# Turning the normalised rows of a macaron block by VectorE block turns and a DRAM scratch instead of on TensorE, with statistics pooled and two attention products on GpSimd

## The chip, the cores and the metric

One core of one Trainium2 chip. The metric is device time in microseconds (us) of one execution of the kernel.

## What is computed

The input x is 16 sequences of 256 rows of 128 features in float32 (4096 rows). Three blocks follow one another, each added to its own input; each begins with a norm of a row (minus its mean, times the reciprocal root of its variance plus 1e-5).

```python
x = x + 0.5 * ffn(layernorm(x))
x = x + attn(layernorm(x))
x = x + 0.5 * ffn(layernorm(x))

def ffn(x):                      # 128 -> 512 -> 512 -> 512 -> 128, weights -1, 0 or 1
    h = silu(tlin(x, w1, s1)) * tlin(x, w2, s2)
    h = gelu(tlin(h, h1, sh1))
    h = gelu(tlin(h, h2, sh2))
    return tlin(h, w3, s3)       # tlin: x @ w.T * s

def attn(x):
    h = layernorm(x) * gamma + beta
    keys, values = h @ Wk.T + bk, h @ Wv.T + bv
    w = exp((keys @ Wka.T + bka) / sqrt(128))
    w = w / cumsum(w, axis=1)
    return cumsum(w * keys, axis=1) * values
```

## The kernel before, in words

The 4096 rows are 8 tiles of 512 rows. A tile goes through the first ffn (t = 0 to 7), the attention (t = 0 to 7) and the second ffn (t = 8 to 15), so there are 16 ffn passes and 8 attention passes, and 24 norms. x is held twice in SBUF: by rows (x_sb, used for the first ffn's norms) and turned, features on the partitions (xt_sb), where all results are added. All 512-column matmuls of an ffn work on turned tiles; each product is made twice, with the rounded activation ("hi") and with the rest ("lo"), against weights that are exact.

A norm n: where the rows are only in xt_sb, TensorE turns them into y_ps (stage u, four 128x128 transposes). VectorE takes statistics of four 128-row blocks (stats, L825), combines them (aggr, L830 and L832) and makes neg_mean and veps (L839, L840). GpSimd makes rstd by a power and nmr = neg_mean * rstd (L362, L364). ScalarE writes the normalised rows z (four activations, L726). TensorE turns z into xt_ps (stage t, transpose4, L462), and ScalarE and VectorE read that bank: xn_hi (L764) and xn_lo (L913) for an ffn, h_t (L767) for attention.

An ffn pass is stage p1.0 to p1.3 (gate and up products, 4 matmuls each), p2.0 to p2.3 and p3.0 to p3.3 (8 each) and p4 (8): 88 matmuls of 512 columns. Between them ScalarE does tanh, high1, gelu2, high2, gelu3, high3 (four each; a high writes the rounded copy), VectorE gate, up (L855, L867) and low1, low2, low3 (L877, the rest after rounding), and dt adds y_ps to xt_sb (L930). p2 and p3 share two banks (hid_ps), so p3.2 can't start before gelu3.0 has read the first.

An attention pass: logits, keys and values on TensorE (L632, L629, L635) out of one bank xt_ps, which also takes the turned z; exp and keys on ScalarE (L776, L772); on VectorE cumsum (L935), two reciprocals (recip, L940), weight (wgt = kw * rcsum, L943), weight_keys (wgt * keys, L947), pool (L951), values (L957) and dt (xt_sb += adelta, L961).

Every engine runs its own list in order. The lists are strings, ORDER for the middle, walked in loops of three steps with two attention passes (a, b), with START, FIRST_STEP and LAST_STEP around them; a step is one ffn pass on TensorE, and AHEAD says for which later tile a stage of that step is. Waits are on semaphores, set inside the stages. SyncE (the queue SP) issues the loads and, from tile 8 on, the stores (L340). GpSimd has little beside its norms: the copies of the weights at the start and two of the low1 (L375).

Of the kernel before, what the change touches and what calls it, by code (L numbers as in the profile page):

```python
# [4 lines left out]
P = 128  # L5
# [27 lines left out]
        "hi:w1 hi:w2 zwait z",  # L33
        "t vec:s1 bits:h1.1 bits:h1.3 tanh.0 tanh.1 tanh.2 high1.0 tanh.3 high1.1 zwait z.0 z.1 high1.2 bits:h2.0 "
# [15 lines left out]
FIRST_STEP = {  # L50
# [6 lines left out]
}  # L57
ORDER = {
# [31 lines left out]
LAST_STEP = {  # L90
    "PE": "p2.0 p2.1 p2.2 p2.3 p4 p3.0 p3.1 p3.2 last:p4a last:p3.0 last:p3.1 last:p4b last:p4c.0 last:p4c.1",
    "ACT": "gelu2.0 gelu2.1 high2.0 high2.1 gelu2.2 high2.2 gelu2.3 high2.3 gelu3.0 high3.0 gelu3.1 high3.1 "
           "gelu3.2 high3.2 last:gelu.0 last:gelu.1",
# [905 lines left out]
```

## Time and profile before

| | before |
|---|---|
| median of 3 runs | 376.88 us (376.24 to 377.13) |
| span of the profiled execution | 374.9 us |
| left around the span, to the median | 2.0 us |
| TensorE busy | 368.0 us (98%) |
| VectorE busy | 321.9 us (86%) |
| ScalarE busy | 314.1 us (84%) |
| GpSimd busy | 52.6 us (14%) |

The profiled execution is one of its own; its time beside its span isn't listed, so the span is set against the median of the runs. Busy time is the union over an engine's instructions, and instructions overlap at their ends, so that the pace of back-to-back instructions is the distance of their starts and is shorter than the duration of one.

### The profile page before, as it was taken

How to read it: one execution, taken by the hardware profiler on the slowest of the kernel's cores; microseconds unless marked ns; L12 is line 12 of the kernel's file. 1: busy time of each engine (PE TensorE's matmuls, PEld its weight loads, DVE VectorE, ACT ScalarE, POOL GpSimd, SP SyncE). 2: the span in 40 equal slices, each digit the busy share in tenths (PEclk: the TensorE clock that was granted, in tenths of full speed). 3: DMA queues.
4: the chain of work that ended last, by engine and by line, in shares of the span. 5: the costliest groups of instructions: out<-in, count | busy, mean ns of one | idle time of the engine just before them, and what ended most of it. 6: DMA issues, size and time to landing. Idle time of an engine off the chain costs nothing.

```text
span 374.9 us, 5278 instructions
## 1 busy us (share of the span) xinstructions
PE 368.0 (98%) x1662; PEld 291.9 (78%) x1662; DVE 321.9 (86%) x713; ACT 314.1 (84%) x549; POOL 52.6 (14%) x67
## 2 busy tenths in 40 slices
PE   7999999999999999999999999999999999999996
PEld 2678888787787877778788787778877778788885
DVE  5898787999999799999988999989799999976733
ACT  4999699989977999798699979967998998686763
POOL 3531101202101202201021120102101210020000
PEclk9999999999999999999999999999999999999999
DMA  7760000000000000000000000000000000000001
GB/s 246 277 265 1 2 0 0 1 2 1 0 2 0 1 2 2 2 0 1 2 0 1 2 1 28 2 28 1 2 29 0 0 30 1 30 1 28 2 0 58
DMA packets 4494, 9.81 MB, mean 26 GB/s; under 512 B 625, under 2 KB 1905, under 8 KB 4209
## 3 DMA queue, kind: packets, MB, share of 16 engines
q1 hardware_dynamic: 3744, 8.65, 6.3%
q10 hardware_dynamic: 720, 0.80, 0.6%
q8 instruction: 15, 0.25, 0.2%
q14 instruction: 15, 0.11, 0.1%
HBM read 7.35 MB, written 2.10 MB: 25 GB/s over the span
## 4 chain that ended last, share of the span: by engine, by line
PE 95%; DMA 2%; DVE 1%; SPq 1%; issue 0%; ACT 0%; ACTq 0%
PE hid_ps L449 60%; PE gate_ps L449 8%; PE y_ps L449 7%; PE up_ps L449 7%; PE xt_ps L462 3%; DMA x_sb<-x 2%; PE y_ps L462 2%; PE xt_ps L632 2%; PE xt_ps L629 2%; PE xt_ps L635 2%; PE up_ps L507 1%; PE gate_ps L507 1%; DVE gate L855 0%; PE xt_ps L449 0%; DVE xt_sb L924 0%
## 5 line engine op out<-in xcount | busy, mean ns | idle before, releaser
L449 PE MATMUL hid_ps<-act_hi,hi_h 128*128 128x512 f32 x480 | 195.6, 408 | 0.0
L449 PE MATMUL hid_ps<-act_lo,hi_h 128*128 128x512 f32 x480 | 186.8, 389 | 0.0
L877 DVE TENSOR_TENSOR act_lo<-full,act_hi 128x512 fp32r<-128x512 f32 x185 | 122.2, 683 | 26.8 <-ACT act_hi L708 24.3
L701 ACT ACTIVATE full<-hid_ps,vec 128x512 f32<-128x512 f32 x123 | 84.4, 686 | 34.9 <-PE hid_ps L449 31.2
L449 PEld LDWEIGHTS hid_ps<-act_hi,hi_h 128*128 128x128 f32 x480 | 90.1, 188 | 22.4 <-issue 4.1
L449 PEld LDWEIGHTS hid_ps<-act_lo,hi_h 128*128 128x128 f32 x480 | 90.2, 188 | 22.1 <-issue 4.3
L708 ACT ACTIVATE act_hi<-full 128x512 fp32r<-128x512 f32 x127 | 78.5, 630 | 2.3
L362 POOL TENSOR_TENSOR rstd<-veps,half 128x4 f32<-128x4 f32 x24 | 35.2, 1467 | 272.5 <-DVE veps L840 272.5
L855 DVE SCALAR_TENSOR_TENSOR gate<-tanh,gate_ps 128x512 f32<-128x512 f32 x60 | 40.6, 679 | 9.2 <-ACT tanh L684 8.6
L684 ACT ACTIVATE tanh<-gate_ps,s_half 128x512 f32<-128x512 f32 x60 | 40.8, 686 | 8.2 <-PE gate_ps L449 8.2
L867 DVE SCALAR_TENSOR_TENSOR full<-up_ps,s_half,gate 128x512 f32<-128x512 f32 x60 | 44.2, 742 | 0.9
L689 ACT ACTIVATE act_hi<-full 128x512 fp32r<-128x512 f32 x60 | 37.3, 621 | 0.2
L940 DVE RECIPROCAL rcsum<-csum 128x256 f32<-128x256 f32 x16 | 27.9, 1743 | 0.0
L449 PE MATMUL gate_ps<-xn_hi,hi_w 128*128 128x512 f32 x59 | 24.7, 419 | 0.0
L726 ACT ACTIVATE z<-y_ps,nmr,rstd 128x128 f32<-128x128 f32 x64 | 24.0, 460 | 0.8 <-POOL nmr L364 0.8
L449 PE MATMUL y_ps<-act_hi,hi_w 128*128 128x512 f32 x60 | 24.2, 403 | 0.0
L449 PE MATMUL y_ps<-act_lo,hi_w 128*128 128x512 f32 x60 | 23.5, 392 | 0.0
L449 PE MATMUL gate_ps<-xn_lo,hi_w 128*128 128x512 f32 x59 | 23.0, 390 | 0.0
L449 PE MATMUL up_ps<-xn_lo,hi_w 128*128 128x512 f32 x59 | 23.0, 390 | 0.0
L449 PE MATMUL up_ps<-xn_hi,hi_w 128*128 128x512 f32 x59 | 23.0, 390 | 0.0
L825 DVE BATCH_NORM_STATS2 stats<-y_ps 128x6 f32<-128x128 f32 x64 | 14.2, 285 | 0.0
L462 PE MATMUL xt_ps<-ident,z 128*128 128x128 f32 x90 | 13.6, 273 | 0.0
(159 smaller groups left out, 397.8 us busy)
## 6 DMA issues: line engine op xcount, KB each, us to landing
xt_sb<-xt SPq DMA_DIRECT2D x1, 2048.0 KB, 10.9
out<-xt_sb SPq DMA_DIRECT2D x7, 256.0 KB, 2.0
x_sb<-x SPq DMA_DIRECT2D x1, 1536.0 KB, 6.6
raw_h<-h2t SPq DMA_DIRECT2D x4, 256.0 KB, 7.3
raw_h<-h1t SPq DMA_DIRECT2D x2, 256.0 KB, 5.9
raw_w<-w2t ACTq DMA_DIRECT2D x1, 256.0 KB, 4.0
raw_w<-w1t SPq DMA_DIRECT2D x1, 256.0 KB, 3.8
raw_h<-h1t ACTq DMA_DIRECT2D x1, 256.0 KB, 6.7
```

The costliest lines, as they stand in the source:

```text
L362: eng.tensor_tensor(rstd[:, :], veps[:, :], half[:, :], ALU.pow).then_inc(s_pow, 1)
L449: mm = eng.matmul(ps, w, a, start=(first and n == 0), stop=(last and n == len(seq_) - 1))
L462: mm = eng.transpose(dst[:, j * P:(j + 1) * P], src[:, j * P:(j + 1) * P], ident[:, :])
L684: eng.activation(tanh_b[m % 2][:, :], gate_home(T, m)[:, :], ACT.Tanh, scale=s1_half[:, m:m + 1]).then_inc(s_tanh, 1)
L689: eng.activation(act_hi[first_act(T)][:, m, :], full1[m % 2][:, :], ACT.Copy).then_inc(s_hi[1], 1)
L701: eng.activation(full23[m % 2][:, :], home23(n, T, m)[:, :], ACT.Gelu, scale=col("sh1" if n == 2 else "sh2", m)).then_inc(s_gelu[n], 1)
L708: eng.activation(act_hi[n][:, m, :], full23[m % 2][:, :], ACT.Copy).then_inc(s_hi[n], 1)
L726: zz = eng.activation(z[:, j * P:(j + 1) * P], norm_blk(kind, t, j), ACT.Identity, bias=nmr[:, j:j + 1], scale=rstd[:, j:j + 1])
L855: eng.scalar_tensor_tensor(gate_b[m % 2][:, :], tanh_b[m % 2][:, :], 1.0, gate_home(T, m)[:, :], ALU.add, ALU.mult).then_inc(s_gate, 1)
L867: eng.scalar_tensor_tensor(full1[m % 2][:, :], up_home(T, m)[:, :], s12_half[:, m:m + 1], gate_b[m % 2][:, :], ALU.mult, ALU.mult).then_in ...
L877: eng.tensor_tensor(act_lo[a][:, m, :], full[m % 2][:, :], act_hi[a][:, m, :].bitcast(F32), ALU.subtract).then_inc(s_lo[n], 1)
L940: eng.reciprocal(rcsum[:, b], csum[:, b]).then_inc(s_rc, 1)
```

## The change

Of the 24 norms, the first three (ffn 0, 1, 2: BY_PE) stay as they were. For the other 21 (13 of an ffn, 8 of attention):

- stage t of TensorE is gone. VectorE turns z in 32x32 blocks into a buffer zt (stage turn, one instruction of 128x512). SyncE then stores zt (256 KB) in a DRAM scratch, waits for it, and reads it back by four DMAs, one for 32 features each, that put the blocks where they belong: the runs are 32 numbers, 128 bytes, 512 of them in each DMA. ScalarE's and VectorE's stages t read the result xnt from SBUF. zt, the scratch and xnt have two buffers.
- the statistics are combined on GpSimd (aggregate): seven small instructions of 128x4 or 128x8, ahead of the power.
- all eight attention passes: weight is kw * keys and is done on GpSimd, weight_keys multiplies it by rcsum on VectorE, and dt (xt_sb += adelta) is done on GpSimd.
- the lists of all engines are written out for each of 16 steps, and GpSimd and SyncE have one too; stages stand in other places than before. The stores stand in SyncE's list between the turns.

```diff
+            def turn(kind, t):                       # SyncE
+                i, use = slot(kind, t)
+                eng.wait_ge(s_turn, turn_of[kind, t] + 1)
+                if use > 0:
+                    eng.wait_ge(s_turned[i], 64 * use)
+                eng.dma_start(turns[i], zt_b[i][:, :]).then_inc(s_parked[i], 16)
+                if use > 0:
+                    before, at = by_dma[turn_of[kind, t] - 2]
+                    eng.wait_ge(*((s_xlo, at) if before == "ffn" else (s_ht, at + 1)))
+                eng.wait_ge(s_parked[i], 16 * (use + 1))
+                blocks = turns[i].rearrange("(s c) (j q r) -> q c j s r", c=32, j=SUB, r=32)
+                for b in range(4):
+                    eng.dma_start(xnt_b[i][32 * b:32 * b + 32, :].rearrange("c (j s r) -> c j s r", j=SUB, r=32),
+                                  blocks[b]).then_inc(s_turned[i], 16)
...
+            def aggregate(n):                        # GpSimd
...
+                eng.wait_ge(s_bn, SUB * n + SUB)
+                eng.tensor_tensor(pair_diff[:, :], stats[:, :, 1], stats[:, :, 4], ALU.subtract).then_inc(s_agg, 1)
+                eng.tensor_tensor(pair_sum[:, :, :], stats[:, :, 1:3], stats[:, :, 4:6], ALU.add).then_inc(s_agg, 1)
+                eng.wait_ge(s_agg, done + 1)
+                eng.tensor_tensor(diff_sq[:, :], pair_diff[:, :], pair_diff[:, :], ALU.mult).then_inc(s_agg, 1)
+                eng.wait_ge(s_agg, done + 2)
+                eng.tensor_scalar(var_part[:, :], pair_sum[:, :, 1], a / P, b, ALU.mult, ALU.add).then_inc(s_agg, 1)
+                eng.wait_ge(s_agg, done + 3)
+                eng.tensor_scalar(diff_part[:, :], diff_sq[:, :], a / 4.0, None, ALU.mult).then_inc(s_agg, 1)
+                eng.tensor_scalar(neg_mean[:, :], pair_sum[:, :, 0], -0.5, None, ALU.mult).then_inc(s_agg, 1)
+                eng.wait_ge(s_agg, done + 5)
+                eng.tensor_tensor(veps[:, :], var_part[:, :], diff_part[:, :], ALU.add).then_inc(s_ve, 1)
...
+                elif stage == "att_weight":          # GpSimd
+                    eng.wait_ge(s_keysb, t + 1)
+                    eng.wait_ge(s_wgk, t + 1)
+                    eng.tensor_tensor(wgt[:, :], kw[:, :], keys[:, :], ALU.mult).then_inc(s_wg, 1)
+                elif stage == "att_dt":              # GpSimd
+                    eng.wait_ge(s_adelta, t + 2)
+                    eng.tensor_tensor(xt_tile(t), xt_tile(t), adelta[:, :], ALU.add).then_inc(s_x2, 1)
...
+                elif stage in ("turn", "att_turn"):  # VectorE
+                    i, use = slot(kind, t)
+                    eng.wait_ge(s_za, norm_of[kind, t] + 2)
+                    if use > 0:
+                        eng.wait_ge(s_parked[i], 16 * use)
+                    eng.transpose(zt_b[i][:, :], z[:, :]).then_inc(s_turn, 1)
...
+                elif stage == "t" and t not in BY_PE:    # ScalarE
+                    i, use = slot("ffn", t)
+                    eng.wait_ge(s_p1, MC * t)
+                    eng.wait_ge(s_turned[i], 64 * (use + 1))
+                    eng.activation(xn_hi[:, :], xnt_b[i][:, :], ACT.Copy).then_inc(s_xhi, 1)
```

The lists of step 1, and VectorE's of step 11 (a stage without a number before it is for the tile that AHEAD gives: z, turn and stats for step + 2, p1, tanh and high1 for step + 1; "a0:" is attention pass 0):

```diff
+    SP     "turn"
+    POOL   "norm"
+    PE     "t 0:p3.2 p1.0 p1.1 0:p3.3 p2.0 p2.1 p4 p2.2 p1.2 p2.3 a0:u p1.3 p3.0 p3.1 p3.2"
+    ACT    "z gelu2.0 0:high3.3 gelu2.1 high2.0 gelu2.2 tanh.2 high2.1 high2.2 gelu2.3 high2.3 high1.0 tanh.3 "
+           "3:t high1.1 gelu3.0 high3.0 gelu3.1 high1.2 high3.1 a0:z gelu3.2 3:tanh.0 high3.2 high1.3 3:tanh.1 "
+           "gelu3.3 high3.3"
+    DVE    "gate.0 0:low3.2 gate.1 turn 0:low3.3 up.0 low2.0 dt up.1 gate.2 low2.1 low2.2 low2.3 a0:stats 3:t "
+           "low1.0 up.2 low3.0 gate.3 low1.1 up.3 a0:turn 4:stats low3.1 low1.2 low1.3 low3.2"
...
+    DVE    "a5:pool a5:values gate.0 dt gate.1 up.0 stats up.1 low2.0 low2.1 a6:cumsum a6:recip.0 turn a7:stats "
+           "low1.0 low2.2 low2.3 gate.2 a6:recip.1 up.2 a7:turn low1.1 gate.3 low3.0 up.3 13:t a6:weight_keys "
+           "low1.2 low3.1 low1.3 a6:pool low3.2 a6:values low3.3"
```

## Rows read from the trace of the kernel before

**Rows 1.** The page's head and first part: busy time of each engine.
```profile
span 374.9 us, 5278 instructions
PE 368.0 (98%) x1662; PEld 291.9 (78%) x1662; DVE 321.9 (86%) x713; ACT 314.1 (84%) x549; POOL 52.6 (14%) x67
```

**Rows 2.** Waits of TensorE, first and last of four: us in total, times, longest.
```profile
PE y_ps L642 <- POOL ident L355: 2.1, 1, 2.1
...
PE gate_ps L507 <- ACT act_hi L689: 0.2, 1, 0.2
```

**Rows 3.** The chain that ended last, us 59.84 to 84.85: start, us, what.
```profile
62.56 1.81 PE hid_ps L449 x8
...
65.29 0.44 PE xt_ps L462 x4
65.72 1.85 PE y_ps L449 x8
...
68.50 0.86 PE xt_ps L632 x2
...
79.38 0.45 PE xt_ps L462 x4
79.82 0.44 PE y_ps L462 x4
80.26 3.66 PE hid_ps L449 x16
```

**Rows 4.** Stretch 60 to 320 us: busy time of each engine (instructions), clock, DMA.
```profile
60.00:320.00 260.00, 260.00 (x1168) 207.05 (x1167) 240.71 (x525) 229.19 (x396) 36.65 (x38) 1.00 0.01 5
```

**Rows 5.** Groups by line and shape: busy us, mean ns of one, idle before.
```profile
L940 DVE RECIPROCAL rcsum<-csum 128x256 f32<-128x256 f32 x16 | 27.9, 1743 | 0.0
L943 DVE TENSOR_TENSOR wgt<-kw,rcsum 128x512 f32<-128x512 f32 x8 | 5.4, 676 | 0.0
L375 POOL TENSOR_TENSOR act_lo<-full,act_hi 128x512 fp32r<-128x512 f32 x2 | 2.6, 1296 | 2.2 <-ACT act_hi L689 2.2
```

**Rows 6.** Timeline of VectorE, us 257.9 to 263: start, us of each piece.
```profile
257.89 0.38 DVE L832 BATCH_NORM_AGGREGATE mv<-stats 128x2 f32<-128x6 f32 x4
...
259.64 0.16 DVE L839 TENSOR_SCALAR neg_mean<-mv 128x4 f32<-128x4 f32 x1
259.71 0.16 DVE L840 TENSOR_SCALAR veps<-mv 128x4 f32<-128x4 f32 x1
259.78 0.68 DVE L877 TENSOR_TENSOR act_lo<-full,act_hi 128x512 fp32r<-128x512 f32 x1
...
261.27 1.88 DVE L877 TENSOR_TENSOR act_lo<-full,act_hi 128x512 fp32r<-128x512 f32 x3
```

**Rows 7.** Timeline of GpSimd, us 258 to 270.
```profile
259.95 1.38 POOL L362 TENSOR_TENSOR rstd<-veps,half 128x4 f32<-128x4 f32 x1 [19.87 <-DVE veps L840]
261.41 0.60 POOL L364 TENSOR_TENSOR nmr<-neg_mean,rstd 128x4 f32<-128x4 f32 x1
268.19 1.01 POOL L362 TENSOR_TENSOR rstd<-veps,half 128x4 f32<-128x4 f32 x1 [6.18 <-DVE veps L840]
269.27 0.20 POOL L364 TENSOR_TENSOR nmr<-neg_mean,rstd 128x4 f32<-128x4 f32 x1
```

**Rows 8.** Timeline of VectorE, us 14 to 20, while GpSimd did L375.
```profile
18.45 1.00 DVE L877 TENSOR_TENSOR act_lo<-full,act_hi 128x512 fp32r<-128x512 f32 x1 [0.26 <-POOL act_lo L375]
```

**Rows 9.** SyncE's store L340 and load L330: ns of the issue min/median/max.
```profile
L340 SPq DMA_DIRECT2D out<-xt_sb x7: 332/332/348, 230.2 to 368.2; - x7
DMA to landing us min/median/max: 2.0/2.0/2.2
L330 SPq DMA_DIRECT2D raw_w<-w3t x1: 657/657/657, 6.0 to 6.0; - x1
```

**Rows 10.** ScalarE's queue of DMAs: whole page, then us 5.0 to 5.4 (packets, MB, share).
```profile
q10 hardware_dynamic: 720, 0.80, 0.6%
q10 hardware_dynamic: 46, 0.01, 10.8%
```

More of the change, by code:

```diff
@@ L49 @@
 )
-FIRST_STEP = {
[6 rows of a table removed]
-}
-ORDER = {
[5 rows of a table removed]
+STEPS = {
+    "SP": (
+        "",
+        "turn",
+        "a0:turn turn",
+        "a1:turn turn",
+        "turn",
+        "a2:turn turn",
+        "a3:turn turn",
+        "turn",
+        "a4:turn turn",
+        "a5:turn store turn",
+        "store turn",
+        "a6:turn store turn",
+        "a7:turn store turn",
+        "store turn",
+        "store",
+        "store",
+    ),
+    "POOL": (
+        "norm",
+        "norm",
+        "a0:norm norm",
+        "a1:norm norm",
+        "a0:weight norm",
+        "a2:norm a0:dt a1:weight norm",
+        "a3:norm a2:weight a1:dt norm",
+        "a2:dt norm",
+        "a4:norm a3:weight a3:dt norm",
+        "a4:weight a5:norm norm",
+        "a4:dt norm",
+        "a5:weight a6:norm a5:dt norm",
+        "a7:norm a6:weight a6:dt norm",
+        "a7:weight a7:dt norm",
+        "",
+        "",
+    ),
[18 rows of a table added]
     ),
     "ACT": (
[10 rows of a table removed]
[43 rows of a table added]
     ),
     "DVE": (
-        "a:stats low2.0 a:aggr t a:veps low2.1 gate.0 up.0 gate.1 up.1 low2.2 gate.2 low1.0 low2.3 dt up.2 low1.1 "
-        "stats gate.3 aggr up.3 veps a:cumsum low3.0 a:recip.0 low1.2 low3.1 low1.3 low3.2 a:recip.1 low3.3",
-        "b:stats a:weight b:aggr t b:veps a:weight_keys low2.0 a:pool gate.0 a:values gate.1 low2.1 a:dt up.0 up.1 "
[6 rows of a table removed]
-    ),
-}
[L90 to L93, printed above, removed]
-    "DVE": "low2.0 low2.1 low2.2 low2.3 low3.0 low3.1 dt low3.2 last:dt.0 last:dt.1",
-}
[39 rows of a table added]
+    ),
+}
 POOL_FIRST = ("norm", 1, 2)
-AHEAD = {"stats": 2, "aggr": 2, "veps": 2, "norm": 2, "zwait": 2, "z": 2, "t": 1, "p1": 1, "tanh": 1, "gate": 1,
-         "up": 1, "high1": 1, "low1": 1, "u": 2, "p4": -1, "dt": -1}
+BY_PE = (0, 1, 2)
+AGGREGATE = 3
+AHEAD = {"stats": 2, "aggr": 2, "veps": 2, "norm": 2, "z": 2, "t": 1, "p1": 1, "tanh": 1, "gate": 1,
+         "up": 1, "high1": 1, "low1": 1, "u": 2, "turn": 2, "p4": -1, "dt": -1, "store": -1}
 def macaron_block(nc, x, xt, w1t, w2t, h1t, h2t, w3t, wkt, wkat, wvt, wkn, vecs, out, seq):
@@ L111, in macaron_block @@
     assert D == P and TOK % seq == 0
-    GROUP, ATT = 3, 2
-    FIRST = 2
-    LOOPS = NT // ATT
-    assert FIRST + GROUP * LOOPS + 2 == 2 * NT
+    assert all(len(steps) == 2 * NT for steps in STEPS.values())
     with ExitStack() as ctx:
@@ L140, in macaron_block @@
         z = sb("z", [P, TOK])
+        zt_b = [sb(f"zt_{i}", [P, TOK]) for i in range(2)]
+        xnt_b = [sb(f"xnt_{i}", [P, TOK]) for i in range(2)]
+        turns = nc.dram_tensor("turns", [2, P, TOK], F32).ap()
         xn_hi = sb("xn_hi", [P, TOK], F32R)
@@ L314, in macaron_block, with schedule, step @@
         block = ctx.enter_context(nc.Block())
+        def schedule(engine, emit, part):
+            def step(i, order):
+                for stage, chunk, t in items(order, i):
+                    emit(stage, chunk, t)
+            if part == "start":
+                step(-1 if engine == "PE" else -2, START[engine][0])
+            if part == "first":
+                step(-1, START[engine][1])
+            if part == "second":
+                step(0, SECOND_LAYER)
+            if part == "rest":
+                for i, order in enumerate(STEPS[engine]):
+                    step(i, order)
         @block.sync
@@ L336, in _, with emit @@
             eng.dma_start(xt_sb[:, :], xt).then_inc(s_xt, 16)
-            for t in range(NT - 1):
-                eng.wait_ge(s_x1, NT + t + 1)
-                eng.dma_start(out[:, t * TOK:(t + 1) * TOK], xt_tile(t)).then_inc(s_out, 16)
+            def turn(kind, t):
[12 more added lines that the diff above has]
+                                  blocks[b]).then_inc(s_turned[i], 16)
+            def emit(stage, chunk, t):
+                if stage in ("turn", "att_turn"):
+                    turn("ffn" if stage == "turn" else "att", t)
+                elif stage == "store":
+                    eng.wait_ge(s_x1, t + 1)
+                    eng.dma_start(out[:, (t - NT) * TOK:(t - NT + 1) * TOK], xt_tile(t)).then_inc(s_out, 16)
+            schedule("SP", emit, "rest")
             for h in range(2):
@@ new lines, in emit @@
+            def emit(stage, chunk, t):
+                if stage in ("norm", "att_norm"):
+                    norm(norm_of["ffn" if stage == "norm" else "att", t])
+                elif stage == "att_weight":
[5 more added lines that the diff above has]
+                    eng.tensor_tensor(xt_tile(t), xt_tile(t), adelta[:, :], ALU.add).then_inc(s_x2, 1)
@@ L434, in _ @@
+            schedule("POOL", emit, "rest")
         @block.tensor
@@ L584, in emit @@
                         p23(int(stage[1]), t, chunk, general)
-                    elif stage in ("t", "att_t"):
-                        n = norm_of["ffn" if stage == "t" else "att", t]
+                    elif stage == "t":
+                        n = norm_of["ffn", t]
                         if n == 0:
@@ L613, in emit @@
                         last_p4_end(chunk)
-                    elif stage == "u" and t >= NT:
+                    elif stage == "u":
                         eng.wait_ge(s_x2, t - NT + 1)
```

163 lines of the change are left out of this document (85 added, 78 removed), and 123 rows, old and new, of tables (FIRST_STEP, ORDER, STEPS).

## The prediction

> **What bounds the kernel now.** I read the page's busy times first: TensorE is busy for 368.0 of 374.9 us, the others have 14% and more left [rows 1]. Busy matmuls are modelled and can hide gaps, so I looked at its waits next: four entries, 3.5 us in all, from the warm-up products (L642) to the second layer of the first tile (L507) [rows 2]. Third, the chain that ended last: between 60 and 85 us it is TensorE without a break [rows 3]; there an ffn product of 8 matmuls takes 1.81 us, so the 88 of a pass take 20 us, and four 128x128 turns take 0.44 to 0.45 us. The reader is to see that each piece starts where the one before ends. So TensorE's queue sets the time, and work taken off it counts in full, as long as nothing else makes it wait. The middle shows how much room there is: of 260 us VectorE is busy 240.7 (93%) and ScalarE 229.2 (88%), and TensorE all the time at a granted clock of 1.00 [rows 4]. Room of 7% on an engine with a fixed order is little: what I add to VectorE's or ScalarE's waits beyond that shows up in TensorE.
>
> **Part 1, TensorE's turns.** 21 of 24 groups of four transposes go, 84 in all. A group is 0.44 to 0.45 us in the chain, and the product behind it takes 1.85 instead of 1.81 us [rows 3], so 0.48 us if that is its doing. 21 x 0.44 = 9.2, 21 x 0.48 = 10.1. I take 9.7 us off. Stage u (turning xt_sb into rows, 16 groups) stays. Nothing else on TensorE gets cheaper: the 1,408 products of the ffn passes and the attention's are the same. So 9.7 us is also about all that can be had.
>
> **Part 2, VectorE.** Per norm it loses four aggregates with a memset (0.38 us) and two small instructions (0.14 us by their starts, 259.64 to 259.78) [rows 6], some 0.55 us. Per attention pass it loses two instructions of 128x512 with two SBUF inputs, like weight's 676 ns [rows 5], at a pace of 0.6 us when back to back (1.88 us for three) [rows 6]. 21 x 0.55 + 16 x 0.6 = 21.2 us off. It gains 21 block turns of 128x512. The trace has no such instruction. Lower bound: the pace of one pass over 512 columns, 0.6 us [rows 6]. Upper bound: the slowest row, the reciprocal, 1743 ns for 256 columns [rows 5], so 3.5 us for 512. A turn reads and writes each number once without arithmetic, so it is nearest to the plain passes: I take 0.65 us, 13.7 us in all. VectorE ends at 321.9 - 21.2 + 13.7 = 314 us of about 365, 86% as before. At the upper bound it would have 60 us more, 374, and be the bound itself.
>
> In the steps where attention is dense it is tighter. Before, two attention passes fall on three steps; a step is then 20.0 + 2 x 0.45 + 0.67 x (3 x 0.86 + 0.9) = 23.2 us of TensorE [rows 3], and VectorE has 93% of it, 21.5 us. By the new lists steps 5 to 12 hold 6.5 passes in 8 steps, 0.81 per step; TensorE's length of a step there is 20.0 + 0.45 + 0.81 x (3 x 0.86 + 0.45) = 22.9 us (0.86 is one attention product, 0.45 a stage u [rows 3]). One pass costs VectorE roughly 10 us (an estimate: reciprocals 3.5, four scans, statistics and four products), so it has 21.5 + 0.14 x 10 - 0.81 x 1.2 = 21.9 us, 96%. It fits, with under 1 us per step to spare.
>
> **Part 3, GpSimd.** Seven small instructions per norm, like nmr: 0.20 us alone, 0.60 when it must share with VectorE [rows 7]; with the power (1.0 to 1.4) and nmr the chain from statistics to z is 7 x (0.2 to 0.35) + 1.4 + 0.3 + waits of some 0.5 = 3.6 to 4.7 us. Before it was 0.5 (VectorE) + 1.7. So z can be written 2 us later. The new lists leave from the end of stats to z at least 3 VectorE instructions and a step's boundary (3 us), mostly 6 us and more. In about five norms ScalarE will wait some 1 us at z. Behind z in its queue are gelu2 and high2 of the tile on TensorE; TensorE has a product of 1.8 us in each of two banks as cover. The two moved products cost 1.30 us each on GpSimd [rows 5]: 16 x 1.3 = 21 us, and GpSimd ends near 53 + 21 + 21 x 2.2 = 120 us, a third of the span. Behind adelta's dt is stage u of the next norm or a store, one pass later than before; wgt is needed half a step later. I cost these at nothing; TensorE's own products cover them.
>
> What GpSimd does to VectorE: while the first of its 1.3 us products ended, a low took 1.00 us in place of 0.68 [rows 8]; beside the power three lows ran at 0.6 us each [rows 6, 7]. So at most 0.3 us for each of the 16 large products, 5 us of VectorE's 51 us room, and nothing for the small ones. The Trainium skill (SBUF — State Buffer, section SBUF: two separate sides) says more: a GpSimd instruction and a VectorE one with two SBUF inputs exclude each other for a whole instruction. By that rule each large product could cost VectorE 1.3 us, 21 us in all, still under its room in the sum; the rows for the small instructions show only GpSimd stretched.
>
> **Part 4, the way through DRAM.** It replaces 0.45 us on TensorE by a delay: block turn, store, read back. The store is like the output's: 2.0 us from issue to landing for the same 256 KB [rows 9]. Then four issues of 0.33 to 0.66 us each [rows 9], and the last lands 2.0 us after its issue if its 512 packets of 128 bytes cost what bytes do. Bounds of a packet: 46 packets, almost all of the 88-byte rows of vecs, took 10.8% of 16 engines in 0.4 us, 15 ns each; all 720 of that queue, 1.1 KB on average, took 0.6% of 374.9 us, 50 ns [rows 10]. At 15 ns the 2048 packets are 1.9 us on 16 engines and hide behind the issues; at 50 ns they are 6.4 us. A turn is then 2.0 + 3 x 0.5 + 2.0 and 0.7 for semaphores and SyncE = 6.2 us, or at the upper end 2.0 + 6.4 + 2.0 = 10.4 us. I take 6.2: the small packets are the nearest row.
>
> What it must fit into: ScalarE's instructions between z and t of the same norm (z as 4). Tile 3: 12; over the 21 norms I count 11 once, 12 three times, 13 four times, then 14 to 27. ScalarE did 396 instructions in 260 us [rows 4], 0.66 us each, so 7.2 us at the least, less 0.65 for the block turn: 6.6 us for a turn of 6.2. It fits even there, if VectorE is on time; in 13 norms there are 2 us and more. Where it doesn't, ScalarE stands at t, and behind it high1 and gelu3, for which p3.2 waits.
>
> **Sum.** The profiled span of 374.9 stands 2.0 us under the median. 376.9 - 9.7 = 367.2. For the waits of parts 2 to 4 (eight tight turns, five tight z, the dense steps), I add 1.5 us, of a range of 0 to 4: **368.7 us**. Own range of this case: 366.3 to 371.5.
>
> **Rivals.** (a) The gain is there but a third or more of it goes into waits of ScalarE and VectorE in the dense steps, where orders are full: 5 to 9 us lost, 371.5 to 376.1. For it: 96% of VectorE. Against: before, 93% left TensorE without any wait [rows 2, 4]. (b) Slower: packets are at the upper end. A turn of 10.4 us exceeds the eight tight places by 10.4 + 0.65 - (11 to 13) x 0.66, 2.5 to 3.8 us each, 25 us, and five others by some 4 us. ScalarE has 12% of room, and half of it, 14 us, reaches TensorE: 376.9 - 9.7 + 14 = 381 us. It decides from some 10 us per turn on, where half the excess passes 9.7 us. The Trainium skill (VectorE: DVE Perf Modes, section The three transpose paths) warns of just this: a plain strided DMA used as a transpose is 19 times slower than the hardware's. Here that would be, from the store's 256 KB in some 0.7 us of moving, 13 us per read-back and well over 400 us in all. Its case is a large innermost stride; here 32 numbers lie together on both sides, and [rows 10] shows 88-byte packets at 15 ns. (c) VectorE becomes the bound: from 1.2 us per block turn on in the dense steps, from 3.1 us everywhere; at 3.5 us about 380 to 385. Against: nothing that only moves data is so slow [rows 5, 6]. (d) The transposes were hidden anyway and nothing changes: against it is the unbroken chain [rows 3].
>
> **Chances.** Forecast 60%; (a) 18%; (b) 12%, a quarter of it within 0.2% of before; (c) 5%; another wait in the new orders that costs over 10 us 3%; under 366.3 us 2%. About 0.2% is what a measurement can tell from no change. Faster 0.80, same 0.04, slower 0.16. Range 366.3 to 376.1: the forecast and (a).
>
> **What would show it.** After, TensorE's busy time is near 358 of a span of 366.7. Right: 12 transposes of z left beside the 64 of xt_sb, VectorE's block turn near 0.65 us, VectorE's busy time near 314, GpSimd's near 120, read-backs landing about 2 us after issue, four of 0.33 to 0.66 us. Wrong, and how: TensorE's hid_ps waiting for ScalarE, which waits for a DMA at its t (b), for GpSimd's nmr at z (part 3), or for VectorE's low (a, c). The prediction falls if TensorE's products themselves slow down, which nothing in the trace suggests.

## The result and the profile after

The median of before is 377.0 us (4 runs), that of after 379.12 us (4 runs, 378.63 to 379.98): a ratio of 1.0061, 95% interval 1.0044 to 1.0078. The change made the kernel 2.1 us slower, where 368.7 us was forecast, and the time is outside the range. The profiled execution of after took 378.93 us, with a span of 377.1 us.

The head and busy times of after, to be held against [rows 1]:

```profile
span 377.1 us, 5304 instructions
PE 365.9 (97%) x1578; PEld 281.0 (75%) x1578; DVE 319.9 (85%) x571; ACT 311.6 (83%) x549; POOL 111.8 (30%) x230
```

The 84 transposes are gone (1662 matmuls, now 1578), but TensorE's busy time fell by 2.1 us and not by 9.7. The ends of matmuls are modelled, so lost time hides in it. The distances between the starts of TensorE's instructions show it: summed over what is beyond the pace of each kind, from 20 us on, they lose 2.7 us before and 13.8 us after (worked out from the two timelines). That is 11.1 us of new gaps, more than the transposes were worth. (An instruction's pace is the usual distance from its start to the next one's; for an ffn matmul it is 0.227 us.) In windows of 20 us the loss is seen even in busy time (before, TensorE was busy for 20.00 us in each of these three):

```profile
60.00:80.00 20.00, 19.13 (x83) 14.73 (x82) 14.91 (x29) 17.16 (x30) 7.03 (x21) 1.00 0.21 41
260.00:280.00 20.00, 18.89 (x82) 14.10 (x80) 18.23 (x33) 17.04 (x29) 6.32 (x12) 1.00 0.19 53
280.00:300.00 20.00, 18.90 (x78) 13.81 (x78) 18.00 (x31) 16.91 (x29) 8.36 (x18) 1.00 0.24 53
```

The granted clock (third column from the end) is 1.00 as in [rows 4], so it is no cause. The waits of all engines in after (us, times, longest):

```profile
ACT full L862 <- PE hid_ps L609: 19.9, 34, 1.9
ACT z L894 <- POOL nmr L552: 15.8, 17, 1.6
DVE zt L1083 <- ACT z L894: 12.3, 10, 2.3
...
PEld hid_ps L609 <- ACT full L862: 7.2, 12, 1.4
PEld hid_ps L609 <- DVE act_lo L1052: 4.0, 10, 0.5
...
ACT h_t L938 <- DMA xnt<-turns: 1.2, 1, 1.2
```

The second line is the new one. Before, ScalarE stood at z for nmr for 1.4 us in all. Now it stands there 17 times, 15.8 us (16 times and 15.2 us at the 21 changed norms; the other wait, 0.6 us, is at the first norm and was there before), and VectorE stands 12.3 us at its block turn for the z that is then late. The first line is ScalarE's cover: before, it had 31.2 us of waits for TensorE; 11 us of them are used up. The last line is all that ScalarE waits for the DRAM route.

The groups and the DMAs of after (busy us, mean ns; KB each, us from issue to landing):

```profile
L1052 DVE TENSOR_TENSOR act_lo<-full,act_hi 128x512 fp32r<-128x512 f32 x185 | 123.7, 695 | 27.8 <-ACT act_hi L869 23.2
L532 POOL TENSOR_TENSOR pair_diff<-stats 128x4 f32<-128x4 f32 x21 | 8.0, 382 | 114.2 <-DVE stats L1000 114.1
L550 POOL TENSOR_TENSOR rstd<-veps,half 128x4 f32<-128x4 f32 x24 | 27.5, 1144 | 10.6 <-DVE veps L1015 7.8
L1083 DVE STREAM_TRANSPOSE zt<-z 128x512 f32<-128x512 f32 x21 | 14.9, 707 | 12.4 <-ACT z L894 12.3
...
turns<-zt SPq DMA_DIRECT2D x21, 256.0 KB, 2.0
xnt<-turns SPq DMA_DIRECT2D x84, 64.0 KB, 2.5
```

**One late z, followed.** The timeline of after around tile 4's norm, GpSimd's and ScalarE's, then TensorE's (start, us):

```profile
57.51 0.58 POOL L532 TENSOR_TENSOR pair_diff<-stats 128x4 f32<-128x4 f32 x1 [3.12 <-DVE stats L1000]
58.04 0.65 POOL L533 TENSOR_TENSOR pair_sum<-stats 128x8 f32<-128x8 f32 x1
58.65 0.64 POOL L535 TENSOR_TENSOR diff_sq<-pair_diff 128x4 f32<-128x4 f32 x1
59.38 0.51 POOL L537 TENSOR_SCALAR var_part<-pair_sum 128x4 f32<-128x4 f32 x1
59.97 0.23 POOL L539 TENSOR_SCALAR diff_part<-diff_sq 128x4 f32<-128x4 f32 x1
60.17 0.22 POOL L540 TENSOR_SCALAR neg_mean<-pair_sum 128x4 f32<-128x4 f32 x1
60.35 0.21 POOL L542 TENSOR_TENSOR veps<-var_part,diff_part 128x4 f32<-128x4 f32 x1
60.69 1.04 POOL L550 TENSOR_TENSOR rstd<-veps,half 128x4 f32<-128x4 f32 x1
61.81 0.20 POOL L552 TENSOR_TENSOR nmr<-neg_mean,rstd 128x4 f32<-128x4 f32 x1
```
```profile
62.04 1.65 ACT L894 ACTIVATE z<-x_sb,nmr,rstd 128x128 f32<-128x128 f32 x4 [1.42 <-POOL nmr L552]
63.60 0.67 ACT L862 ACTIVATE full<-hid_ps,vec 128x512 f32<-128x512 f32 x1
```
```profile
63.06 0.39 PE L609 MATMUL hid_ps<-act_lo,hi_h 128*128 128x512 f32 x1
64.32 0.50 PE L609 MATMUL hid_ps<-act_hi,hi_h 128*128 128x512 f32 x1 [0.87 <-ACT full L862]
```

The statistics were done at 57.43. Seven small instructions, the power and nmr take until 62.01, 4.58 us. ScalarE had nothing else to do from 60.62 and stood 1.42 us at z. Behind z in its list is a gelu, which starts at 63.60 and frees the bank; TensorE starts its product at 64.32, 1.03 us behind its pace of 0.23 us. So 1.03 us of the 1.42 us at z come out at TensorE within one product.

**All of them.** For each of the 21 norms I took two times from the timelines of after: the chain, from the end of stats to the end of nmr, and the room, from the end of stats to where ScalarE stands at z. In 16 norms the room is 2.6 to 4.4 us, mean 3.5, and the chain 3.0 to 5.4 us, mean 4.2. Three more (room 5.9 to 12.9 us) are fine. In the last two, a weight stands ahead of the norm in GpSimd's list and waits for keys; z waits 1.63 and 1.04 us there.

### The profile page after: what moved, and what is told of

It is laid out like the page before. It is cut to its first block and busy times, and to the rows that moved or that the text cites. A ratio compares the mean times of both kernels' runs of the same rounds, so it can differ in the third digit from the quotient of the medians.

```text
span 377.1 us, 5304 instructions
## 1 busy us (share of the span) xinstructions
PE 365.9 (97%) x1578; PEld 281.0 (75%) x1578; DVE 319.9 (85%) x571; ACT 311.6 (83%) x549; POOL 111.8 (30%) x230
## 3 DMA queue, kind: packets, MB, share of 16 engines
q1 hardware_dynamic: 51120, 19.67, 19.4%
## 5 line engine op out<-in xcount | busy, mean ns | idle before, releaser
L609 PE MATMUL hid_ps<-act_hi,hi_h 128*128 128x512 f32 x480 | 192.0, 400 | 2.2 <-ACT full L862 2.2
L1052 DVE TENSOR_TENSOR act_lo<-full,act_hi 128x512 fp32r<-128x512 f32 x185 | 123.7, 695 | 27.8 <-ACT act_hi L869 23.2
L532 POOL TENSOR_TENSOR pair_diff<-stats 128x4 f32<-128x4 f32 x21 | 8.0, 382 | 114.2 <-DVE stats L1000 114.1
L550 POOL TENSOR_TENSOR rstd<-veps,half 128x4 f32<-128x4 f32 x24 | 27.5, 1144 | 10.6 <-DVE veps L1015 7.8
L609 PE MATMUL gate_ps<-xn_hi,hi_w 128*128 128x512 f32 x59 | 26.0, 440 | 0.0
L1083 DVE STREAM_TRANSPOSE zt<-z 128x512 f32<-128x512 f32 x21 | 14.9, 707 | 12.4 <-ACT z L894 12.3
L588 POOL TENSOR_TENSOR xt_sb<-xt_sb,adelta 128x512 f32<-128x512 f32 x8 | 10.7, 1341 | 47.6 <-DVE adelta L1141 47.6
```

What stands on the lines that cost most here:

```text
L550: eng.tensor_tensor(rstd[:, :], veps[:, :], half[:, :], ALU.pow).then_inc(s_pow, 1)
L609: mm = eng.matmul(ps, w, a, start=(first and n == 0), stop=(last and n == len(seq_) - 1))
L1052: eng.tensor_tensor(act_lo[a][:, m, :], full[m % 2][:, :], act_hi[a][:, m, :].bitcast(F32), ALU.subtract).then_inc(s_lo[n], 1)
L1083: eng.transpose(zt_b[i][:, :], z[:, :]).then_inc(s_turn, 1)
```

## The experiments

Seventeen kernels ran. Theory A of the expectations is the late z: the chain on GpSimd is longer than the room, and the lists have no slack behind z. Its rivals are the way through DRAM, the two products moved to GpSimd with what they cost VectorE, and the fullness of VectorE and ScalarE. "Gaps" is TensorE's loss worked out as above (before 2.7, after 13.8 us); "z" is ScalarE's wait at z for nmr.

| run | median us | ratio to before (95%) | z us | gaps us |
|---|---|---|---|---|
| after | 379.12 | 1.0061 (1.0044 to 1.0078) | 15.8 | 13.8 |
| e1 statistics on VectorE | 373.36 | 0.9907 (0.9892 to 0.9922) | 0.4 | 7.7 |
| e2 short chain | 369.97 | 0.9812 (0.9799 to 0.9826) | 2.6 | 5.5 |
| e3 z and turn later | 386.80 | 1.0273 (1.0247 to 1.0299) | 1.5 | 21.8 |
| e4 products on VectorE | 386.22 | 1.0245 (1.0231 to 1.0259) | 14.8 | 21.6 |
| e5 two small ones on VectorE | 376.82 | 0.9997 (0.9982 to 1.0013) | 10.1 | 10.5 |
| e6 four on VectorE | 374.20 | 0.9925 (0.9911 to 0.9940) | 4.1 | 8.9 |
| e7 two more small ones | 388.05 | 1.0309 (1.0280 to 1.0338) | 23.7 | 22.0 |
| e8 e2 with stage u doubled | 377.78 | 1.0025 (1.0015 to 1.0035) | 1.1 | 3.5 |
| e9 before, statistics on GpSimd | 376.93 | 1.0004 (0.9995 to 1.0014) | 1.6 | 3.1 |
| e10 turn later | 388.03 | 1.0289 (1.0245 to 1.0333) | 13.4 | 22.1 |
| e11 z one later | 378.55 | 1.0045 (1.0031 to 1.0059) | 3.4 | 13.2 |
| e12 low with one input | 369.61 | 0.9807 (0.9792 to 0.9822) | 5.0 | 5.0 |
| e13 no wait for the store | 378.51 | 1.0052 (1.0037 to 1.0067) | 15.6 | 13.3 |
| e14 e1 with e13 | 373.32 | 0.9899 (0.9880 to 0.9918) | 0.6 | 7.7 |
| e15 e2 with e13 | 369.02 | 0.9805 (0.9789 to 0.9821) | 1.5 | 3.9 |
| e16 stats earlier | 377.20 | 1.0020 (1.0009 to 1.0031) | 12.5 | 12.0 |
| e17 e16, norm before weight | 376.38 | 0.9993 (0.9984 to 1.0003) | 9.7 | 10.7 |

### The chain on GpSimd, longer and shorter

**e1** puts the statistics back on VectorE, for all 21 norms; the arithmetic is complete.

```diff
-                if n >= AGGREGATE:               # GpSimd
-                    aggregate(n)
+                if n >= AGGREGATE:               # VectorE, behind stats
+                    norm_aggr(n)
+                    norm_veps(n)
```

> The statistics of the 21 later norms are combined on VectorE again (four aggregates, neg_mean, veps right behind stats, two buffers for each); all else is the changed kernel's, 379.1 us. Theory A, the chain: seven small instructions on GpSimd take 1.5 us alone and up to 4 us when each waits for a VectorE product, so that z comes some 1 us late at 15 norms, ScalarE stands there, and TensorE after it; without them z is on time: 371 to 374 us, ScalarE's waits at z under 3 us (15.8 before). Theory B, full lists: VectorE and ScalarE have no room in the dense steps, and VectorE gets 11 us more here: 380 us or more.

373.36 us, 5.8 us faster than after and 3.5 faster than before, with VectorE busier (329.5 us) than in either. The chain is 2.1 to 2.6 us in all norms but three, against the same rooms.

**e2** makes the chain three small instructions. It leaves out of the variance the part that comes from the difference of the two half-rows' means.

```diff
-                eng.tensor_tensor(pair_diff[:, :], stats[:, :, 1], stats[:, :, 4], ALU.subtract)
...
-                eng.tensor_tensor(veps[:, :], var_part[:, :], diff_part[:, :], ALU.add).then_inc(s_ve, 1)
+                eng.tensor_scalar(veps[:, :], pair_sum[:, :, 1], a / P, b, ALU.mult, ALU.add).then_inc(s_ve, 1)
```

> GpSimd makes only three of the seven small instructions of each norm (the sum of the halves, neg_mean, veps); the part of the variance that comes from the difference of the halves' means is left out. VectorE and ScalarE do the same as in the changed kernel. Theory A: the chain is 1 to 2 us shorter, 372 to 375 us, waits at z under 4 us. Theory B: nothing was taken off a full engine, 378 us or more.

369.97 us, near the forecast of 368.7 and below the 372 to 375 us that theory A gave for this run. Its busy times and its two waits around z:

```profile
PE 360.6 (98%) x1578; PEld 282.4 (77%) x1578; DVE 318.1 (86%) x571; ACT 311.6 (85%) x549; POOL 91.6 (25%) x146
```
```profile
DVE zt L1076 <- ACT z L887: 3.9, 7, 1.2
ACT z L887 <- POOL nmr L545: 2.6, 5, 1.2
```

In the 16 tight norms the chain is 3.05 us on average and the room as before, 3.5. Four instructions fewer are worth 9.2 us, everything else being the same: the lists, the route, the block turns, the moved products.

**e5 and e6** take two (difference and sum of the halves) and four of the seven to VectorE, the arithmetic complete. **e7** adds two small instructions to the seven, whose results nothing uses.

```diff
+                for of in (extra_a, extra_b):        # e7, GpSimd
+                    eng.tensor_tensor(of[:, :], stats[:, :, 1], stats[:, :, 4], ALU.subtract)
```

> Complete statistics; of the seven small instructions the first two (difference and sum of the halves) are made by VectorE right behind stats, five stay on GpSimd, and the power and nmr behind them. The changed kernel is 379.1, the short chain (three small ones) 370.0 us. Theory A, each GpSimd instruction in the chain costs some 2.3 us of the whole: 374 to 376 us. Theory B, room on VectorE counts most: it gets 3 us more, so 379 us or more.

> Complete statistics; four of the small instructions (sum, difference, neg_mean, the part of the variance within the halves) are VectorE's, three stay on GpSimd. Theory A: the chain on GpSimd is as long as in the short chain, VectorE has some 6 us more, 370 to 372.5 us, less than with all statistics on VectorE (373.4) and below the kernel before (376.75). Theory B: 373.5 us or more.

> The changed kernel with two more small instructions at the head of GpSimd's chain (the difference made three times). Theory A: another 3 to 6 us, 382 to 385 us. If the chain is not what decides: 379 us.

The waits at z go 4.1, 10.1, 15.8, 23.7 us for three, five, seven and nine small instructions on GpSimd, and the time 374.2, 376.8, 379.1, 388.1 us. The order is theory A's; its sizes are not. e5 came out above the 374 to 376 us expected, e7 above the 382 to 385, and e6 in the range that was theory B's, 373.5 us or more. Only e2 and e7 change the chain and nothing on VectorE: each of the four that e2 leaves out is worth 2.3 us over 21 norms, each of the two that e7 adds 4.5 us, where z is already late. e6 and e2 leave the same number on GpSimd; the four that e6 does on VectorE (9 us more, 327.1 against 318.1) cost 4.2 us. That is about the price of VectorE's fullness here; 1.5 us more of waits at z are in it.

### Is the saving on TensorE there at all?

**e8** is e2 with each group of four transposes of stage u done twice: 16 groups, 7.0 us more on TensorE by [rows 3].

```diff
+                        for j in range(SUB):
+                            eng.transpose(y_ps[:, j * P:(j + 1) * P], xt_tile(t)[:, j * P:(j + 1) * P], ident[:, :])
                         transpose4(y_ps, xt_tile(t), s_u)
```

> The short chain (370.0 us) with the four transposes of stage u made twice, 16 groups of 0.44 us more on TensorE. If TensorE's queue sets the time again once the chain is short: 7 us more, 376.5 to 377.5 us. If waits still do: 371 to 374 us.

7.8 us slower than e2, where 7.0 were added and 376.5 to 377.5 us expected; the 0.8 us over is not explained. With z in time, TensorE's queue sets the time as before, and its instructions count in full.

### The moved products

**e4** gives weight and att_dt back to VectorE and keeps the rest.

```diff
-        "a2:norm a0:dt a1:weight norm",              # GpSimd's list
+        "a2:norm norm",
```

> The two attention products (weight and dt) are back on VectorE, weight right before weight_keys, dt right behind values; statistics stay on GpSimd. Theory C, large GpSimd products block VectorE (one low took 1.60 us beside one): 16 blocks of up to 0.9 us go, 9.6 us of VectorE work come: about 379 us. Theory A: z waits remain, 379 to 381 us. Theory B: VectorE is fuller, 382 us or more.

386.22 us: the moved products are not the cause of the loss but worth 7 us where they are. That is theory B's range (382 us or more); A and C had given 379 to 381. The waits at z stay (14.8 us). TensorE's for lows grow, from 4.0 and 3.4 us to 6.4 and 6.1. Busy time alone doesn't explain the 7 us: e1, with z in time, has VectorE busy for 329.5 us and takes 373.36 us, e4 328.7 and 386.22. How much of it is the late z and how much the place of the two products in VectorE's list was not tested.

### The same chain on the old lists

**e9** is the kernel before with nothing but the aggregate of the change on GpSimd.

> One part alone: the kernel before, with its lists and its turns on TensorE, and only the statistics of norms 3 to 23 combined on GpSimd (seven small instructions, as in the changed kernel). Theory A, the chain: it is 2 to 4 us longer than the 1.7 us that these lists were made for; z and what is behind it in ScalarE's list come late: 380 to 388 us, waits at z over 10 us (1.4 before). If the chain hurts only together with the way through DRAM: 376 to 378 us, since VectorE gets 11 us of room.

```diff
             def norm_aggr(n):                        # and norm_veps alike
+                if n >= AGGREGATE:                   # GpSimd does aggregate(n) ahead of the power
+                    return
```

No difference, where theory A had forecast 380 to 388 us. The forecast took the chain of these lists for 1.7 us. That is GpSimd's part of it; the trace of before, read as above, has 3.0 to 7.9 us from the end of stats to the end of nmr (mean 5.0), because aggr and veps stand behind other instructions in VectorE's list. One of these norms (VectorE, GpSimd twice, ScalarE):

```profile
69.81 0.87 DVE L825 BATCH_NORM_STATS2 stats<-x_sb 128x6 f32<-128x128 f32 x4
...
72.19 0.16 DVE L840 TENSOR_SCALAR veps<-mv 128x4 f32<-128x4 f32 x1
```
```profile
72.43 1.31 POOL L362 TENSOR_TENSOR rstd<-veps,half 128x4 f32<-128x4 f32 x1 [10.25 <-DVE veps L840]
73.82 0.57 POOL L364 TENSOR_TENSOR nmr<-neg_mean,rstd 128x4 f32<-128x4 f32 x1
```
```profile
77.47 1.64 ACT L726 ACTIVATE z<-x_sb,nmr,rstd 128x128 f32<-128x128 f32 x4
```

The chain is 3.7 us here and the room 6.9. Over the 21 norms of before the room is 4.1 to 15.2 us, mean 6.5. In e9 the chain is 3.1 to 4.7 us, mean 3.9, about as in after; the shortest rooms are two of 4.1 us, the next five 4.4 to 4.7, and z waits 1.6 us in all. So theory A holds only with its second half. The chain alone costs nothing, and it is not longer than before's was; what the change took away is the room, from 6.5 us on average to 3.5 in 16 norms. e9 also says that taking 21 aggregates off VectorE (314.3 us) gains nothing where TensorE's queue sets the time.

### Moving stages in the lists

**e3** moves z two places later in ScalarE's list and the block turn two later in VectorE's, at 15 norms; **e10** the block turn alone; **e11** z alone, by one.

```diff
-        "z gelu2.0 0:high3.3 gelu2.1 high2.0 ..."
+        "gelu2.0 0:high3.3 z gelu2.1 high2.0 ..."    # e3
-        "gate.0 0:low3.2 gate.1 turn 0:low3.3 up.0 ..."
+        "gate.0 0:low3.2 gate.1 0:low3.3 up.0 turn ..."    # e3, e10
```

> Same work, other order: in 15 norms z stands two instructions later in ScalarE's list, and the block turn two later in VectorE's. Theory A: the waits at z, 15.8 us in all, are filled with other work: 374 to 377 us. If instead the place of z was right and any delay of it is passed on to the tile's p1, it stays at 379 or gets slower. Theory B: 379 us, the same waits at another place.

> The changed kernel (379.1) with the block turn two places later in VectorE's list at 15 norms, z where it was. If the way through DRAM has some us of room behind it, as with a landing well before stage t: 379 to 380 us. If it has less than 1 us at several norms: 382 us or more, ScalarE waiting for the read-back; then most of the 7.7 us of z and turn moved together is this.

> The changed kernel with z one place later in ScalarE's list at 15 norms, about the 0.9 us that it waits on average, the block turn where it was. Theory A, the wait at z itself is the loss: 376 to 378 us. If what counts is when z is written, and not what ScalarE does until then: 379 us or a little more.

The waits at z go down to 1.5 us in e3, and the time gets worse by 7.7 us, where theory A had 374 to 377 us. The lateness has moved on:

```profile
ACT xn_hi L872 <- DMA xnt<-turns: 8.3, 8, 3.0
DVE xn_lo L1043 <- ACT xn_hi L872: 7.7, 6, 3.6
...
PE y_ps L571 <- ACT z L843: 3.6, 2, 1.9
...
PE gate_ps L558 <- ACT xn_hi L872: 2.9, 2, 2.3
```

e10 shows the same with z where it was: ScalarE waits 10.3 us at xn_hi for the read-back. In e11 the wait at z goes from 15.8 to 3.4 us, but VectorE's at the block turn rises from 12.3 to 15.0, and stage u waits 2.5 us for the bank that z reads; the median is 0.6 us lower, which the intervals don't tell from nothing. So there is no room behind z either: the path from stats by z, block turn and DRAM to xn_hi is tight from end to end, and filling a wait with other work brings nothing while z is written as late.

**e16** goes to the other end and keeps all the work: stats stands one or two places earlier at five norms where its input had been ready. **e17** also puts the norm ahead of weight in GpSimd's list, at two places.

```diff
-        "... low2.2 low2.3 a0:stats 3:t low1.0 up.2 low3.0 gate.3 low1.1 up.3 a0:turn 4:stats ..."
+        "... low2.2 a0:stats low2.3 3:t low1.0 up.2 low3.0 gate.3 low1.1 4:stats up.3 a0:turn ..."
...
-        "a2:norm a0:dt a1:weight norm",              # e17, GpSimd
+        "a2:norm a0:dt norm a1:weight",
```

> The kernel after with nothing but VectorE's stats moved in its lists: two places earlier for tiles 3 and 4, one place for attention 0 and for the norms of steps 6 and 7, where its input had been ready. The trace of after gives the room of these norms, from the end of stats to where ScalarE stands at z: 3.64, 3.87, 3.19, 3.27 and 3.43 us, against a chain on GpSimd of 4.84, 4.43, 4.58, 4.12 and 2.99 us. If it is the room that is short, four of these z start 0.6 to 1.5 us earlier against the rest, ScalarE's wait at z for nmr falls from 15.8 us to some 12 us, and the time from 379.1 to 376 to 377.5 us. If full engines are the cause and the wait at z only shows it, the instructions of VectorE that now come behind stats are 0.8 us later, TensorE waits for these, and the time stays at 379 us or rises.

> As the run before it, and in GpSimd's list the norm stands ahead of weight at two places (of tile 6 with attention 1, and of attention 5 with attention 4), where weight stood waiting for keys with the statistics of the norm long done: z waited 1.63 and 1.04 us there. If late z's are the cause, ScalarE's wait at z falls by another 2.7 us, to some 9 us, and the time by another 1 to 2 us, to 374.5 to 376.5 us. If fullness is the cause: no change to the run before it, or a rise by the 1 us that weight is later.

Both came out as the late z has it. e16's and e17's waits:

```profile
ACT z L843 <- POOL nmr L501: 12.5, 14, 1.6
```
```profile
ACT z L843 <- POOL nmr L501: 9.7, 12, 1.3
```

At the first three of these norms the room grew to 5.1 to 5.4 us and the wait is gone; at the fourth the small instructions fell beside other work of VectorE, the chain grew with the room, to 4.9 us, and the 0.9 us stayed. By the ratios 1.5 us were gained by e16 and 1.0 more by e17, without an instruction fewer, and TensorE's gaps fall from 13.8 to 12.0 and 10.7 us. Little more can be had this way: in most of the other norms that need stage u, stats starts within 0.5 us of its end on TensorE, or waits for it.

### The way through DRAM

**e13** takes the store's wait out of the route: the read-back comes from a weight's rows in DRAM, with the same pattern, and the turned rows are not used. **e14** and **e15** do the same to e1 and e2.

```diff
-                eng.wait_ge(s_parked[i], 16 * (use + 1))
-                blocks = turns[i].rearrange("(s c) (j q r) -> q c j s r", c=32, j=SUB, r=32)
+                blocks = w1t.rearrange("(s c) (j q r) -> q c j s r", c=32, j=SUB, r=32)
```

> The changed kernel (379.1 us), but the read-back fetches 128x512 numbers of another DRAM tensor (w1t), so it doesn't wait for the store to land, 1.7 us less from the block turn to stage t; the stores are still made. The turned rows are therefore not used. If the route as a whole is short of time: 372 to 375 us. If only z's place in ScalarE's list is: 377.5 to 379 us, and the waits at z stay at 15 us.

> As before, on the kernel with all statistics on VectorE (373.4 us), where no z waits for GpSimd. If the route is what holds: 370 to 372 us. If VectorE's fullness is: 373 us.

> As before, on the short chain (370.0 us). If there is still some of the route in its 370: 368 to 369 us. If it is TensorE's queue again: 369.5 to 370 us.

From the store's issue to the last landing the route takes 5.0 us in e13 and 6.6 in after. These 1.6 us bring 0.3 us by the ratio in each of the three, less than half the width of one interval, and the waits at z stay at 15.6 us in e13. The DRAM end is not where after loses its time.

### What stretches GpSimd's small instructions

The timelines of GpSimd and VectorE in after, us 119 to 126:

```profile
119.35 0.20 POOL L532 TENSOR_TENSOR pair_diff<-stats 128x4 f32<-128x4 f32 x1 [21.54 <-DVE stats L1000]
...
119.94 0.74 POOL L537 TENSOR_SCALAR var_part<-pair_sum 128x4 f32<-128x4 f32 x1
120.77 0.56 POOL L539 TENSOR_SCALAR diff_part<-diff_sq 128x4 f32<-128x4 f32 x1
...
124.17 1.29 POOL L588 TENSOR_TENSOR xt_sb<-xt_sb,adelta 128x512 f32<-128x512 f32 x1
```
```profile
119.19 0.85 DVE L1000 BATCH_NORM_STATS2 stats<-x_sb 128x6 f32<-128x128 f32 x4
119.96 2.48 DVE L1052 TENSOR_TENSOR act_lo<-full,act_hi 128x512 fp32r<-128x512 f32 x4
...
124.63 1.38 DVE L1052 TENSOR_TENSOR act_lo<-full,act_hi 128x512 fp32r<-128x512 f32 x1
```

Beside stats a small instruction takes 0.20 us. From the moment the lows run it takes 0.56 to 0.74, about the pace of a low: it seems to get its turn between two of them. But nmr, at 124.02 in the same trace, takes 0.20 us again, beside a reciprocal.

The whole trace of after says which VectorE instructions do this. Of its 171 small instructions on GpSimd (seven in each of 21 norms, and 24 nmr), 95 overlap no VectorE instruction with two SBUF inputs. They take 0.19 to 0.23 us, every one: 80 of them beside gates, ups, reciprocals or stats, 15 beside nothing. The other 76 run beside a low, a scan, weight_keys or xn_lo from SBUF; they take 0.50 us on average and up to 0.75, and 59 of them over 0.3 us. In e2, e7, e9 and e16 the first kind is likewise never over 0.24 us.

The other way, a low took 1.38 us beside the 1.29 us of L588, in place of 0.68. Three lows of after started in the middle of one of the 16 large products, and all three took 1.34 to 1.60 us; gates, ups and reciprocals beside these products kept their times. The longest:

```profile
236.56 1.30 POOL L588 TENSOR_TENSOR xt_sb<-xt_sb,adelta 128x512 f32<-128x512 f32 x1 [3.00 <-DVE adelta L1141]
```
```profile
236.82 1.60 DVE L1052 TENSOR_TENSOR act_lo<-full,act_hi 128x512 fp32r<-128x512 f32 x1 [0.33 <-ACT act_hi L869]
```

The Trainium skill (SBUF — State Buffer, section SBUF: two separate sides) describes this, a lock that is held for a whole instruction, between a GpSimd instruction that reads SBUF and a VectorE instruction that has two SBUF inputs or runs in one of its two-port performance modes. The trace agrees for the two SBUF inputs, in both directions.

**e12** makes low from one SBUF input, so its value is not the rest after rounding.

```diff
-                eng.tensor_tensor(act_lo[a][:, m, :], full[m % 2][:, :], act_hi[a][:, m, :].bitcast(F32),
-                                  ALU.subtract).then_inc(s_lo[n], 1)
+                eng.tensor_scalar(act_lo[a][:, m, :], full[m % 2][:, :], 0.0, 0.0, ALU.mult,
+                                  ALU.add).then_inc(s_lo[n], 1)
```

> The changed kernel with each low on VectorE as an instruction with one SBUF input (full * 0 + 0 in place of full - act_hi; the rest after rounding is left out). If GpSimd's small instructions wait for VectorE instructions with two SBUF inputs: their mean falls from 0.35 to 0.2 us, waits at z fall under 4 us, 370 us or less. If any VectorE instruction holds them up: means stay above 0.3 us. Should the new form also be shorter than 0.6 us, VectorE is lighter, and the time alone doesn't tell, but the means do.

369.61 us, but the time says nothing on the lock: low also became shorter, and VectorE less full (275.1 us).

```profile
L1052 DVE TENSOR_SCALAR act_lo<-full 128x512 fp32r<-128x512 f32 x185 | 76.6, 429 | 45.4 <-ACT act_hi L869 35.7
```
```profile
L532 POOL TENSOR_TENSOR pair_diff<-stats 128x4 f32<-128x4 f32 x21 | 6.0, 287 | 121.7 <-DVE stats L1000 121.7
```

GpSimd's small ones fell from means of 304 to 404 ns to 225 to 328, not to 200, and the waits at z to 5.0 us, not under 4. The new low is the reason: of the small instructions that overlap it and no instruction with two inputs, the mean is 0.31 us and the longest 0.59, and one such low took 1.14 us beside a weight:

```profile
182.91 1.28 POOL L585 TENSOR_TENSOR wgt<-kw,keys 128x512 f32<-128x512 f32 x1
```
```profile
183.33 1.14 DVE L1052 TENSOR_SCALAR act_lo<-full 128x512 fp32r<-128x512 f32 x1
```

The 91 that overlap neither take 0.19 to 0.24 us. So a low with one input still excludes GpSimd, while the other one-input instructions don't. It differs from them in its pace: 0.43 us for 512 columns, where the plain passes of before take 0.6 or more. That fits the two-port mode in the Trainium skill's sentence above, but no run here has such a low at the plain pace.

## Why the prediction was wrong

**Part 1, right.** 84 transposes are gone and worth what was said, once nothing else is late: e2 is 7.0 us faster than before with 2.8 us of extra gaps, and e8 shows TensorE's queue setting the time.

**Part 2, right in its prices.** The block turn takes 0.71 us (taken 0.65). VectorE's busy time is 319.9 us in place of 314: 1.2 us are the block turns, 2.2 us the lows (695 ns, before 683, x185), and the rest was not traced to its instructions. A fuller VectorE does cost time: e1, with 11 us more of it, takes 3.4 us longer than e2, and e6 4.2 us. The 7 us of e4 are not of this alone.

**Part 3, the step that failed.** The chain was forecast at 3.6 to 4.7 us and measures 3.0 to 5.4, mean 4.2: nearly right. The room was not: "at least 3 VectorE instructions and a step's boundary (3 us), mostly 6 us and more". It is 2.6 to 4.4 us in 16 of 21 norms. I had read the room off the order of VectorE's list alone; what counts is when ScalarE, on its own list, comes to z. The comparison with before was wrong too, "0.5 (VectorE) + 1.7": there the chain took 5.0 us on average, in a room of 6.5. So the sentence "In about five norms ScalarE will wait some 1 us at z" should have read 16 waits of 0.95 us. Two were not of this kind: GpSimd's own list had a weight ahead of the norm, which stood under "I cost these at nothing" (e17, 1.0 us).

**What a late z costs, also wrong.** "TensorE has a product of 1.8 us in each of two banks as cover": the followed z shows that this cover is spent when ScalarE stands at z, since ScalarE is only just ahead. And z is waited for three times: by ScalarE's gelus, by VectorE at the block turn with its lows behind it, and by stage u for the bank. 15.8 us of waits at z came with 11.1 us of gaps. In the sum, 1.5 us for waits of parts 2 to 4 stood where 11 belong. 9.2 to 9.7 saved less 11.1 is a loss of 1.4 to 1.9 us; 2.1 were measured. Of the 11.1 us some 8 go with the long chain; e2, with z nearly in time, keeps 2.8 us, which alone would have been within the prediction's 0 to 4.

**GpSimd's load, right in the sum.** It is busy for 111.8 us (forecast 120), its products take 1.3 us each. Of "at most 0.3 us for each of the 16", three met a low, at 0.65 to 0.92 us each, 2.2 us in all: more each and fewer than said.

**Part 4, right.** Store 2.0 us, issues of 0.63 us (taken 0.5), landing 2.5 us (taken 2.0): some 6.6 us per turn from the store's issue to the last landing, against 6.2. ScalarE waited for it once, 1.2 us. The upper end of 50 ns per packet and rival (b) fall: SyncE's queue carried 51,120 packets in 19.4% of 16 engines' 377.1 us, against 3,744 in 6.3% before, so that the 47,376 new ones took 17 ns each, near the lower bound of 15. The factor of 19 that the Trainium skill (VectorE: DVE Perf Modes, section The three transpose paths) gives for a plain DMA transpose is for a large innermost stride of the destination. Here runs of 32 numbers lie together on both sides, so no run tests it. The tightness counted there was real, though, and e3 and e10 ran into it.

**The rivals.** (a) had the right kind, waits of ScalarE and VectorE in full lists, but at 5 to 9 us, and named VectorE's fullness where the late z came first. (c) fell; so did (d), with e2 and e8. "Another wait in the new orders that costs over 10 us", at 3%, is what came.

**What stays open.** What e4's 7 us consist of, and whether the one-input low of e12 excludes GpSimd because of its faster mode. And whether lists exist in which the whole path, from stage u to xn_hi, fits with the statistics on GpSimd: e3, e10, e11, e16 and e17 each moved only some stages. The fastest version with complete arithmetic that ran is e1, 373.36 us.

## What to carry to other kernels

When a step of a chain that crosses engines is moved to a slower one, work out for every occurrence two numbers from the timelines, before and after: the chain's length, and the room until the consumer's engine stands at it on its own list. Here the chain was no longer than before (4.2 us against 5.0); the new order had cut the room, from a mean of 6.5 us to 3.5 in 16 of 21 norms. With full lists on both sides most of a lateness can come out at the bound engine (11.1 us of gaps beside 15.8 us of waits at z), and other engines wait for the same tile too. To see what an order can give, try it at both ends: later consumers (e3, e10, e11) brought nothing, since there was no room behind them, earlier producers (e16, e17) helped at once. And place GpSimd's small instructions beside VectorE instructions that have at most one SBUF input.

## What the runs showed of the hardware

- A GpSimd instruction of 128x4 or 128x8 took 0.19 to 0.23 us where it overlapped no VectorE instruction with two SBUF inputs (95 in after, 80 of them beside gates, ups, reciprocals or stats), and 0.50 us on average, up to 0.75, when it overlapped one with two SBUF inputs (76). The smallness of an operation says little about its latency on GpSimd; its neighbour on VectorE does.
- A VectorE product with two SBUF inputs took 1.34 to 1.60 us when it started in the middle of a GpSimd product of 128x512 (three times), in place of 0.68. A one-input low at the fast pace of 0.43 us took 1.14 us.
- VectorE's block turn of 128x512 in float32 took 0.71 us, about the time of a plain pass.
- A read-back of 64 KB in 512 runs of 128 bytes took 0.63 us to issue and 2.5 us to land; the packets that the way through DRAM added took 17 ns each.
